# Key-length term of a sixteen-head attention: from diagonal matmuls to scaled table blocks that TensorE turns into the score banks

## The reference

```
dt   = |t_i - t_j|
E    = exp(clip(-mu*dt, -30, 0))                      # by head and distance
s    = einsum('bihd,bjhd->bhij', qr, conj(kr)).real
qn   = |q|^2 summed over the head,  kn = |k|^2 summed over the head
maha = max(qn_i + E*E*kn_j - 2*E*s, 0) / V            # V by head and distance
logits = coef * log1p(maha/nu) - 0.5*64*log(V)
A    = softmax(causal logits);   out = A @ v;   y = out @ Wo
```

## Time and profile before

| | us |
|---|---|
| median of 3 runs | 3072.42 (3070.5 to 3085.04) |
| profiled execution | 3083.46 |
| its span, first to last instruction | 3082.2 |
| heads at their steady pace | 1690.56 to 3046.73 |
| mean granted TensorE clock | 0.972 of full |

### The profile page before, as it was taken

How to read it: one execution, slowest core, us unless ns; L and a number is a source line. 1 busy time by engine, 2 the same in 40 slices (tenths; PEclk the granted TensorE clock), 3 DMA queues, 4 the chain that set the end, 5 groups by cost and what they waited for, 6 DMA issues and landing times. The chain is left out here.

```text
span 3082.2 us, 55344 instructions
## 1 busy us (share of the span) xinstructions
PE 2946.1 (96%) x19062; PEld 2235.2 (73%) x19062; DVE 2434.7 (79%) x4760; ACT 1807.0 (59%) x4118; POOL 884.1 (29%) x839
## 2 busy tenths in 40 slices
PE   6999998999999999999687999999999999999998
PEld 4777775566666677787575787877878777878777
DVE  5878876566557555456766999999999999999997
ACT  3455544655645444434464777677777676776776
POOL 2111101101101100000433444444444444444442
PEclk8999999999999899999898999999999999999999
DMA  2000001000000000000402223232232323223221
GB/s 57 2 5 15 28 15 52 1 1 1 1 1 1 1 1 1 1 1 1 115 1 55 49 59 76 58 73 49 57 76 59 76 59 76 58 50 76 47 49 44
DMA packets 79513, 111.66 MB, mean 36 GB/s; under 512 B 15942, under 2 KB 32521, under 8 KB 79241
## 3 DMA queue, kind: packets, MB, share of 16 engines
q1 hardware_dynamic: 75266, 105.77, 14.3%
q10 hardware_dynamic: 3974, 2.37, 0.3%
HBM read 34.43 MB, written 6.55 MB: 13 GB/s over the span
## 5 line engine op out<-in xcount | busy, mean ns | idle before, releaser
L3346 DVE CUSTOM_DVE_ANT_0 scratch<-scratch,tb,coef 128x512 f32<-128x512 f32 (+3 forms) x512 | 552.9, 1115 | 1.3 <-ACT scratch L3418 1.3
L75 PE MATMUL banks<-lower 128*128 128x128 f32 (+2 forms) x2688 | 510.6, 356 | 1.4 <-DMA lower<-in_L_w2T 0.8
L75 PEld LDWEIGHTS banks<-lower 128*128 128x128 f32 (+1 forms) x2688 | 346.3, 195 | 166.4 <-issue 165.2
L75 PEld LDWEIGHTS banks<-scratch,tb 128*128 128x128 f32 x2560 | 357.3, 192 | 101.9 <-issue 61.9
L75 PE MATMUL banks<-scratch 128*128 128x256 f32 (+3 forms) x1088 | 378.1, 433 | 11.4 <-ACT scratch L3026 8.9
L3511 POOL TENSOR_TENSOR normed<-normed,aT 128x512 f32<-128x512 f32 x128 | 176.7, 1381 | 709.4 <-DVE aT L3304 426.0
L75 PE MATMUL banks<-scratch,tb 128*128 128x128 f32 x2560 | 369.4, 275 | 0.0
L75 PEld LDWEIGHTS banks<-n,pt 128*128 128x128 f32 x2560 | 300.8, 192 | 54.8 <-ACT pt L3440 51.1
L75 PE MATMUL banks<-n,pt 128*128 128x128 f32 x2560 | 323.5, 278 | 3.1 <-ACT moe L3459 3.1
L83 DVE SCALAR_TENSOR_TENSOR scratch<-scratch,tb 128x512 f32<-128x512 f32 (+3 forms) x512 | 320.8, 656 | 2.3
L83 DVE SCALAR_TENSOR_TENSOR scratch<-tb,nn,banks 128x512 f32<-128x512 f32 (+3 forms) x512 | 263.7, 535 | 41.1 <-PE banks L75 41.1
(11 more groups left out here) (433 smaller groups left out, 5448.3 us busy)
## 6 DMA issues: line engine op xcount, KB each, us to landing
scratch<-normed SPq DMA_DIRECT2D x512, 128.0 KB, 2.4
tb<-head_rows SPq DMA_DIRECT2D x32, 512.0 KB, 8.5
turn<-head_turns SPq DMA_DIRECT2D x32, 128.0 KB, 3.5
xs<-in_x SPq DMA_DIRECT2D x8, 256.0 KB
head_turns<-loads SPq DMA_DIRECT2D x8, 256.0 KB, 2.5
head_turns<-rotation SPq DMA_DIRECT2D x8, 256.0 KB, 2.8
w<-in_L_Wqk SPq DMA_DIRECT2D x8, 256.0 KB, 3.2
out<-xs SPq DMA_DIRECT2D x8, 256.0 KB, 2.3
```

The lines of the kernel that those rows point to most:

```text
L75: return self.T.matmul(out, lhsT, rhs, start=start, stop=stop, skip_group_check=True)
L3346: x = V.tensor_tensor_reduce(y, y, view(hd["tb"][:, e, 2, i * P + 127:i * P + 128], [[-1, n]]), k.coef[:, h:h + 1], 3e38, ALU.add, ALU.min ...
```

## The change

The key-length term is made another way. The fourth table is now spread over the partitions from offset 0 instead of 384, so that, read backwards, row p of it is the table for key p. For each key block j, one instruction multiplies this row with the length of key p (a scalar per partition) for all the query blocks that the key block meets: 512, 384, 256 and 128 columns for j = 0 to 3. GpSimd makes the widest (`first_keys`, tb scaled into `gk[0]`), ScalarE the other three (`key_norms`). `scores` first has TensorE transpose these blocks straight into the score bank, then lets the query-key matmul accumulate on top. The constant `backwards`, the diagonals `dk` and POOL's `norms` are gone, and `square` no longer writes the keys reversed. There is one set of `gk` per head instead of four sets of `dk`: a unit's blocks can be written only after the last scores of the same head in the pair before. The fourth table has a DMA of its own, so a head pair's tables come in 6 DMAs instead of 4. The loops of all four engines are written in another order.

```
         def scores(g, p):
+            k.after(T, k.h_gk, g + 1)
             k.after(T, k.h_dk, g + 1)
...
-            at = 0
+            rows, at = [], 0
             for i in k.PIECES[p]:
-                n = (i + 1) * P
-                ps = k.bank(4 + e)[:, at:at + n]
-                k.mm(ps, r["qk"][:, 0, e, i * P:(i + 1) * P], r["qk"][:, 1, e, 0:n], stop=False)
+                rows.append((i, k.bank(4 + e)[:, at:at + (i + 1) * P]))
+                at += (i + 1) * P
+            for i, ps in rows:
                 for j in range(i + 1):
-                    x = k.mm(ps[:, j * P:(j + 1) * P], hd["tb"][:, e, 3, (i - j) * P:(i - j + 1) * P],
-                             t["dk"][:, 3 - j, :], start=False)
-                at += n
+                    k.tr(ps[:, j * P:(j + 1) * P], t["gk"][j][:, (i - j) * P:(i - j + 1) * P],
+                         start=(i == rows[0][0] and j == 0))
+            for i, ps in rows:
+                x = k.mm(ps, r["qk"][:, 0, e, i * P:(i + 1) * P], r["qk"][:, 1, e, 0:(i + 1) * P], start=False)
...
+        def key_norms(g):
...
+            k.after(A, k.h_nn, m + 1)
+            if m:
+                k.after(A, k.h_sc, k.pieces(m - 1, 2, e))
...
+            for j in range(1, TPB):
+                x = A.activation(t["gk"][j], view(hd["tb"][:, e, 3, S - 1:S], [[-1, (TPB - j) * P]]),
+                                 ACT.Identity, scale=r["nn"][:, j, 2 + e:3 + e])
+            x.then_inc(*k.h_dk.up())
...
-        def norms(g):
+        def first_keys(g):
...
             k.after(G, k.h_nn, m + 1)
-            k.after(G, k.h_sc, 6 * (m - 1))
-            G.tensor_tensor(t["dk"][:, :, :], k.backwards[:, :].unsqueeze(1).broadcast_to([P, 4, P]),
-                            r["nn"][:, :, 2 + e].unsqueeze(2).broadcast_to([P, 4, P]), ALU.mult).then_inc(*k.h_dk.up())
+            if m:
+                k.after(G, k.h_sc, k.pieces(m - 1, 2, e))
...
+            k.ts(t["gk"][0], view(hd["tb"][:, e, 3, S - 1:S], [[-1, S]]), r["nn"][:, 0, 2 + e:3 + e],
+                 eng=G).then_inc(*k.h_gk.up())
...
         for m in range(-4, k.PAIRS + 1):
+            scores(2 * m + 2, 2)
             scores(2 * m + 3, 2)
...
+            flip(2 * m + 1, 2)
             scores(2 * m + 4, 0)
             scores(2 * m + 5, 0)
+            scores(2 * m + 4, 1)
             values(2 * m, 2)
```

More of the change, by code:

```diff
@@ L2672, in load_tables @@
         for e in range(2):
-            for first in (0, 2):
-                k.Y.dma_start(k.head[j]["tb"][:, e, first:first + 2, :],
-                              k.spread(2 * hp + e, first, 2, 384)).then_inc(*k.h_tb[j].up(16))
+            for first, n, at in ((0, 2, 384), (2, 1, 384), (3, 1, 0)):
+                k.Y.dma_start(k.head[j]["tb"][:, e, first:first + n, :],
+                              k.spread(2 * hp + e, first, n, at)).then_inc(*k.h_tb[j].up(16))
     def move(self, m, x):
@@ L3266, in heads_pe @@
             values(2 * m - 1, 2)
-            flip(2 * m, 2)
+            scores(2 * m + 2, 2)
             scores(2 * m + 3, 2)
             sums(m + 2)
+            flip(2 * m, 2)
             project(m + 3, 1)
@@ L3315, in query_norms @@
             if m % SEQS == 0:
[L3316 removed]
+                V.wait_ge(k.h_tb[m // SEQS % 2].sem, 96 * (m // SEQS // 2 + 1))
             k.after(V, k.h_fl, 3 * (g - 4) + p + 1)
@@ L3358, in heads_dve @@
         for m in range(-4, k.PAIRS + 1):
-            query_norms(2 * m + 3, 1)
-            products(m + 3, 0, 1)
+            logits(2 * m + 1, 2)
             distance(2 * m + 3, 1)
-            reciprocals(2 * m)
             query_norms(2 * m + 2, 2)
-            distance(2 * m + 2, 2)
-            query_norms(2 * m + 3, 2)
             logits(2 * m + 2, 0)
             logits(2 * m + 3, 0)
+            query_norms(2 * m + 3, 2)
+            distance(2 * m + 2, 2)
             products(m + 3, 1, 1)
-            query_norms(2 * m + 4, 0)
             distance(2 * m + 3, 2)
@@ L3372, in heads_dve @@
             logits(2 * m + 2, 1)
-            query_norms(2 * m + 5, 0)
+            query_norms(2 * m + 4, 0)
             logits(2 * m + 3, 1)
             logits(2 * m + 2, 2)
-            reciprocals(2 * m + 1)
+            query_norms(2 * m + 5, 0)
             distance(2 * m + 4, 0)
+            reciprocals(2 * m)
             query_norms(2 * m + 4, 1)
             distance(2 * m + 5, 0)
+            products(m + 4, 0, 0)
+            products(m + 4, 0, 1)
+            query_norms(2 * m + 5, 1)
+            reciprocals(2 * m + 1)
             distance(2 * m + 4, 1)
-            logits(2 * m + 3, 2)
-            products(m + 4, 0, 0)
     def heads_act(self):
@@ L3392, in square @@
             k.after(A, k.h_nl, m)
-            out = view(k.squares[1][:, 0, S - 1:S], [[S, 2], [-1, S]]) if x else k.squares[0]
-            A.activation(out, r["qk"][:, x, :, :], ACT.Square).then_inc(*(k.h_sk if x else k.h_sq).up())
+            A.activation(k.squares[x], r["qk"][:, x, :, :], ACT.Square).then_inc(*(k.h_sk if x else k.h_sq).up())
         def lengths(m):
@@ L3408, in norms @@
             k.after(A, k.h_dk, 2 * (m - 1))
+            k.after(A, k.h_gk, 2 * (m - 1))
             k.after(A, k.h_qn, 6 * (m - 1))
             A.activation(r["nn"][:, :, :], k.bank(1).rearrange("p (i c w) -> p i c w", i=TPB, c=4)[:, :, :, 0], ACT.Identity).then_inc(*k.h_nn.up())
+        def key_norms(g):
+            if not 0 <= g < k.UNITS:
+                return
+            m, e, t, r, hd = k.unit(g)
+            k.after(A, k.h_nn, m + 1)
+            if m:
+                k.after(A, k.h_sc, k.pieces(m - 1, 2, e))
+            if m % SEQS == 0:
+                A.wait_ge(k.h_tb[m // SEQS % 2].sem, 96 * (m // SEQS // 2 + 1))
+            for j in range(1, TPB):
+                x = A.activation(t["gk"][j], view(hd["tb"][:, e, 3, S - 1:S], [[-1, (TPB - j) * P]]),
+                                 ACT.Identity, scale=r["nn"][:, j, 2 + e:3 + e])
+            x.then_inc(*k.h_dk.up())
         def logarithm(g, p):
@@ L3464, in heads_act @@
         for m in range(-4, k.PAIRS + 1):
+            exponential(2 * m + 1, 1)
+            logarithm(2 * m + 3, 0)
+            turned(2 * m, 0)
+            lengths(m + 2)
+            exponential(2 * m, 2)
+            logarithm(2 * m + 2, 1)
+            outputs(2 * m - 1)
+            norms(m + 2)
+            turned(2 * m, 1)
+            turned(2 * m, 2)
             exponential(2 * m + 1, 2)
+            key_norms(2 * m + 4)
+            turned(2 * m + 1, 0)
             logarithm(2 * m + 3, 1)
-            norms(m + 2)
             logarithm(2 * m + 2, 2)
-            turned(2 * m, 2)
+            key_norms(2 * m + 5)
+            exponential(2 * m + 2, 0)
+            turned(2 * m + 1, 1)
             values(2 * m + 1)
-            outputs(2 * m - 1)
-            exponential(2 * m + 2, 0)
-            turned(2 * m + 1, 0)
             exponential(2 * m + 3, 0)
-            turned(2 * m + 1, 1)
             square(m + 3, 0)
-            outputs(2 * m)
             logarithm(2 * m + 3, 2)
@@ L3481, in heads_act @@
             logarithm(2 * m + 4, 0)
-            exponential(2 * m + 3, 1)
+            outputs(2 * m)
             values(2 * m + 2)
             square(m + 3, 1)
[L3485 to L3490, removed]
     def heads_pool(self):
         k, G = self, self.G
-        def norms(g):
+        def first_keys(g):
             if not 0 <= g < k.UNITS:
@@ L3527, in heads_pool @@
         for m in range(-4, k.PAIRS + 1):
+            accumulate(2 * m - 2)
             rotate(m + 3, 0)
-            norms(2 * m + 4)
-            norms(2 * m + 5)
+            first_keys(2 * m + 4)
+            first_keys(2 * m + 5)
             rotate(m + 3, 1)
             accumulate(2 * m - 1)
-            accumulate(2 * m)
     def heads_close(self):
```

28 lines of the change are left out of this document (14 added, 14 removed).

## The result

The changed kernel takes 2967.84 us (median of 4 runs, 2963.38 to 2975.98), against 3075.39 of the kernel before in the same comparison: ratio 0.965, 95% interval 0.9617 to 0.9682. 2946 was predicted, with a range of 2926 to 3014. The profiled execution took 2963.38 us, its span is 2961.7, 120.5 us less than the span before.

A forecast was written before the change was run, and what follows sets the result against it. PE was taken to bound the kernel at 22.28 us a turn, DVE close behind; PE would allow 20.05, DVE some 20.3, so 1.98 us times 64 saves 127 us: 2946 us against the median, range 2926 to 3014.

The forecast's parts named there:

- TensorE's saving: On PE, 20 key-length blocks a turn as transposes save 2.23 us, taking its turn from 22.28 to 20.05 us.
- DVE takes over the turn: On DVE, less holding by POOL takes busy time from 21.90 to 20.3 us, just above PE's 20.05.
- my list: DVE instructions held by POOL in a turn before the change: customs and the `distance` pair, 6.1 us in all.
- the smaller `distance`: On DVE, a smaller `distance` that met POOL too was to give back about 0.3 us a turn.
- The scaling on POOL: POOL's two new 512-column scalings would take 1.0 us each, replacing two instructions of 1.25 us.
- The rule that I had read from the additions: DVE instructions with two SBUF operands wait for the POOL instruction under way; those with a PSUM operand do not.
- slower, from about 2.0 us per scaling: Rival, 3%: POOL scalings of 2.5 us hold DVE's customs of 512, making the turn 23.3 us and the time 3137 us.
- The order: Moving `accumulate` and the query products changes which DVE instructions meet POOL: terms of -1.0, -1.1 and +0.8 us a turn.
- Waits added: Scalings wait for the same head's last scores; PE has some 7.0 us of other work before needing new blocks.
- DMA: Table loads per head pair rise from 4 to 6, issued by SP with four turns of lead; cost nothing.
- ACT: On ScalarE, six added scalings a turn take 2.0 us, from 15.7 to 17.7, costed at nothing as covered.
- The clock: Rival, 2%: PE drops to 1.2 GHz among the transposes, +2.8 us a turn, 3250 us.

The follow-up runs named there:

- e_mm: The changed kernel with the scaled blocks brought into the score banks by ordinary matmuls against the identity: 3076.72 us, ratio 0.9993 to the kernel before.
- e_turned2: The changed kernel with a second `turned` buffer and semaphore, so queries and keys have one each: 2938.48 us, ratio 0.9559 to the kernel before.
- e_double: The changed kernel with GpSimd doing each scaling twice, the extra result into memory nobody reads: 2988.7 us, ratio 0.9706 to the kernel before.
- e_mech: The changed kernel with the old order of all four loops: 2984.4 us, ratio 0.9687 to the kernel before.
- e_order: The kernel before, its key-length term unchanged, with the new order of all four loops: 3075.62 us, ratio 0.9989.
- e_both: The changed kernel with all scalings on ScalarE and a second `turned` buffer: 2947.31 us, ratio 0.9583 to the kernel before.

## Why the prediction came out right, and where it was off

**What bounds the kernel, and TensorE's saving: right.** 0.111 us a block and 2.23 us a turn were predicted; turned back into matmuls the kernel is where it was (e_mm), and with nothing else in the way the turn is 20.01 us (e_turned2) for the 20.05 worked out.

**DVE takes over the turn at some 20.3 us: right in the number.** It is 20.27, with DVE busy throughout. The sum of held time is 4.9 us: two customs of 128 (1.0 each), one of 256 (0.35), one of 512 (0.43), the `distance` pair (2.33 - 0.61 = 1.7), one `distance` of 384 (0.41). Before it was 6.5 and not 6.1, since my list had left out the `distance` of 384, held in that turn too:

```profile
2033.13 0.93 DVE L83 SCALAR_TENSOR_TENSOR scratch<-scratch,tb 128x384 f32<-128x384 f32 x1
```

So DVE's own work is 15.4 us, and 15.4 + 4.9 = 20.3. The custom of 384 went free as forecast, and the customs of 512 gave back 1.2 for the 1.1 forecast. Two smaller terms were off and cancelled: the pair gained 0.6 instead of 0.8, and the smaller `distance` gave back nothing instead of 0.3. That part of the number is luck. So is the alignment: with the buffer of its own DVE needs only 19.3 us (e_turned2), and in the turns of 20.01 it has time to spare, so 20.27 is DVE's only after the shift.

**The scaling on POOL: wrong in size, and its rival was wrong in kind.** It takes 1.6 us, not 1.0 (2262.29 to 2265.47 for two). By my sum, 0.6 us more on each of two should have cost DVE about 1.2 us a turn. It did not, since the instruction holds DVE only for its first 0.6 us; doubling the scalings added nothing to DVE's busy time (e_double). The rule that I had read from the additions, that DVE waits for the whole POOL instruction, does not hold for this one. The rival "slower, from about 2.0 us per scaling" rested on a price for held time that this instruction does not have.

**The order: its weight was overrated.** I credited the order with making DVE fit. With the old one the mechanism alone already gives 2984 us (e_mech), 94 us less than the kernel before; the order is worth some 15 us of the 108 to 110, and nothing without the transposes (e_order).

**The term left out: the DMAs of queries and keys.** Under "Waits added" and "DMA" the prediction went through `gk` and the table loads, and not through the waits of `products` for `h_mv`. In the kernel before, the last DMA landed 1.9 us (median) ahead of the queries' product and 2.2 ahead of the keys'. With the new mechanism in the old order it is 1.9 and 0.8 (e_mech), in the changed kernel 0.4 and 0.8, and in its turns of 20.01 the keys' product starts as soon as the last DMA has landed. So the new order took the room at the queries' product, and at the keys' product the new mechanism took it already in the old order. Four such DMAs usually take 4.15 us from the first issue to the last landing, and up to 6.2 us. Late ones are not new: 28 of 107 groups were over 4.4 us in the kernel before, 23 of 117 in the changed one. Less than half of these overlap the loads of weights or tables (9 of the 23); what delays the rest is open. They cost 11.7 us of waits, and bring the kernel from turns of 20.01 to turns of 20.27 (0.26 x 58 = 15 us). Together that is near the 24 us that the second buffer gives back.

**ACT: right.** 17.94 us against 17.7, and no harm. ACT's last block ends 0.70 us before PE's first transpose for the second head (about 1 us was forecast); since PE starts 0.25 us behind a block it waits for (e_both), 0.45 us of that is room, less than the 0.71 us of one more block of 512 columns.

**The clock: right.** 1.00 with 44 transposes a turn, at most seven in a row. The sentence cited as a rival from "TensorE: Matmul & The Clock Gate", Part 4, of the Trainium skill, that the full clock does not engage for transpose mode, found no support here.

**The forecast of 2946 is 22 us under the median.** Against the profiled execution it is 7 us: 2956 for 2963.4, the longer turns. The other 14 come from the step to the median: the profile before lay 11 us above the median that stood on record then, the profile after 4 us below its own. That is spread between runs and says nothing of the mechanism.

The version with the lowest median is e_turned2, 2938.48 us, 4.4% less than the kernel before and 0.8% less than the changed one in the same comparison.

## What to carry to other kernels

When one engine is full and another is at 98%, work out for the second how much of its busy time is its own; instructions that wait for a shared resource look busy. A step that an order moves earlier must be checked for every wait it carries, down to buffers that a DMA empties: at zero slack one late transfer can leave the whole pipeline shifted for good, and a second buffer is then worth more than the waits that one can count. When a gain is suspected to come from several edits at once, take back the one that carries the arithmetic first: e_mm settled the main question in one run.

## What the hardware showed that I had not expected

- A POOL instruction with two SBUF inputs (1.3 us for 512 columns) holds a DVE instruction with two SBUF operands until it ends. One with a single input and a scalar per partition (1.6 us for 512 columns) holds it only for its first 0.6 us (0.43 us lost at 0.14 us into it), and not at all in the cases seen where DVE starts 0.61 us into it or later. Where a DVE instruction with two SBUF operands is still running as the scaling starts, it is the scaling that grows, up to 1.94 us, and then a DVE instruction that starts 0.43 us into it is held too.
- That scaling takes 1.56 to 1.94 us for 512 columns, 1.56 where no such DVE instruction stands in its way, more than a two-input addition (1.28 to 1.46) and more than twice a copy (0.61).
- The same program settles in one of two regular turns, 20.01 or 20.27 us, by a shift of some 0.4 us between DVE and POOL (the scaling 0.28 us behind the second custom of 512, or 0.14 ahead of it); the first late DMA takes it from the one to the other, and in two profiled executions it did not come back.
